# Turning the order of the maxima units and spreading V's products over the period, in a fused attention and mixture-of-experts kernel

## What is computed

```python
q = _apply_rope(q, cos, sin); k = _apply_rope(k, cos, sin)
scores = jnp.einsum('bhsd,bhtd->bhst', q, k) / scale
scores = jnp.where(causal, scores, -inf)
attn = softmax(scores)
out = jnp.einsum('bhst,bhtd->bhsd', attn, v)
```

## Time and profile before

| | |
|---|---|
| median of 3 runs | 180.74 us (180.57 to 181.24) |
| profiled execution, its own time | 180.87 us |
| its span in the trace | 179.1 us |
| busy in the span | PE 95%, VectorE 77%, ACT 75%, POOL 52% |
| granted TensorE clock | 1.00 in every slice |
| attention periods 1 to 6 | 34.67 to 83.47 us |

### The profile page before, as it was taken

How to read it: one execution, slowest core, us unless ns; L and a number is a source line. 1 busy time by engine, 2 the same in 40 slices (tenths; PEclk the granted TensorE clock), 3 DMA queues, 4 the chain that set the end, 5 groups by cost and what they waited for, 6 DMA issues and landing times.

```text
span 179.1 us, 3277 instructions
## 1 busy us (share of the span) xinstructions
PE 169.9 (95%) x944; PEld 117.8 (66%) x944; DVE 138.5 (77%) x444; ACT 134.6 (75%) x224; POOL 93.2 (52%) x117
## 2 busy tenths in 40 slices
PE   6999999899999999988999999987999999999992
PEld 2766675565666666654648777855777877788881
DVE  5598989889898989981586998898699748657561
ACT  3559267687777888889735696944979999999970
POOL 5507187985453969597541632004569941777000
PEclk9999999999999999999999999999999999999999
DMA  5924673677686657521120899970680000001001
GB/s 126 310 48 100 180 197 88 213 264 267 173 239 202 186 183 187 151 88 43 59 55 9 214 322 354 344 216 9 170 297 3 0 4 0 0 2 59 0 4 59
DMA packets 15349, 24.28 MB, mean 136 GB/s; under 512 B 2844, under 2 KB 4828, under 8 KB 15308
## 3 DMA queue, kind: packets, MB, share of 16 engines
q1 hardware_dynamic: 14532, 23.29, 42.9%
q10 hardware_dynamic: 800, 0.79, 1.6%
HBM read 18.71 MB, written 5.27 MB: 134 GB/s over the span
## 4 chain that ended last, share of the span: by engine, by line
PE 77%; DVE 10%; ACT 5%; POOL 3%; issue 3%; DVEq 0%; POOLq 0%
PE psum L1544 12%; PE psum L1545 11%; PE psum L1546 11%; PE psum L1411 10%; PE psum L1471 8%; PE psum L1447 7%; PE psum L1290 4%; PE psum L1356 2%; PE psum L1342 2%; ACT t_probs L1109 2%; DVE psum L776 2%; PE psum L1406 1%; PE psum L1451 1%; DVE t_raw L928 1%; PE psum L1300 1%
## 5 line engine op out<-in xcount | busy, mean ns | idle before, releaser
L776 DVE CUSTOM_DVE_ANT_0 psum<-psum,t_causal 128x128 f32<-128x128 f32 (+3 forms) x128 | 58.5, 524 | 5.7 <-PE psum L1411 3.0
L1109 ACT ACTIVATE t_probs<-psum 128x1024 f32<-128x1024 f32 (+2 forms) x48 | 40.9, 884 | 8.2 <-PE psum L1447 5.2
L1411 PE MATMUL psum<-t_stacked,t_q_pad 96*128 96x256 f32 (+2 forms) x104 | 33.3, 391 | 0.5 <-DMA t_q_pad<-scratch 0.2
L1411 PEld LDWEIGHTS psum<-t_stacked,t_q_pad 96*128 96x128 f32 x104 | 18.4, 189 | 12.4 <-DVE t_row_max L776 10.1
L948 DVE SCALAR_TENSOR_TENSOR t_q_pad<-psum,t_zw_all,t_q_pad 128x512 fp32r<-128x512 f32 x24 | 17.8, 748 | 9.9 <-ACT t_q_pad L1157 9.9
L676 POOL TENSOR_SCALAR_AFFINE_SELECT t_probs<-t_probs 128x512 f32<-128x512 f32 x32 | 20.4, 649 | 9.0 <-ACT t_probs L1109 9.0
L1143 ACT ACTIVATE psum<-psum 128x512 f32<-128x512 f32 x40 | 23.5, 587 | 0.4 <-DVE t_q_pad L951 0.2
L707 POOL TENSOR_TENSOR t_q_pad<-t_raw,t_q_pad 128x512 fp32r<-128x512 f32 x8 | 10.3, 1294 | 21.6 <-ACT t_q_pad L1159 21.6
L1471 PE MATMUL psum<-t_probs,t_v_all 128*32 128x512 f32 (+3 forms) x256 | 20.6, 439 | 0.0
L776 DVE DVE_READ_ACCUMULATOR2_ANT t_row_max<- 128x1 f32 x128 | 18.0, 140 | 0.0
L1157 ACT ACTIVATE t_q_pad<-psum,t_zw_all 128x512 fp32r<-128x512 f32 x24 | 16.6, 691 | 0.9 <-PE psum L1546 0.2
(11 more groups left out here) (233 smaller groups left out, 372.0 us busy)
## 6 DMA issues: line engine op xcount, KB each, us to landing
t_stacked<-scratch SPq DMA_DIRECT2D x16, 256.0 KB, 5.8
t_probs<-in_L_ffn_Wa SPq DMA_DIRECT2D x2, 1024.0 KB, 12.4
scratch<-t_o_sb SPq DMA_DIRECT2D x7, 256.0 KB, 2.0
t_raw<-in_experts SPq DMA_DIRECT2D x7, 256.0 KB, 3.1
t_stacked<-scratch SPq DMA_DIRECT2D x9, 192.0 KB, 3.4
t_q_pad<-scratch SPq DMA_DIRECT2D x28, 48.0 KB
scratch<-t_dn_hi SPq DMA_DIRECT2D x2, 512.0 KB, 3.3
t_q_two<-scratch SPq DMA_DIRECT2D x5, 192.0 KB, 2.5
```

The costliest lines, as they stand in the source:

```text
L776: last = V.tensor_tensor_reduce(scores, scores, causal[:, S - width:S], 1.0, 3 * BIG, ALU.add, ALU.max, row_max[s][:, qb, j:j + 1])
L1109: A.activation(o, scores, ACT.Exp, scale=float(1.0 / np.sqrt(np.float32(HD)))).then_inc(exp_done, 1)
L1411: last = T.matmul(bank[:, o:o + width], q_pad[s][0:TOP, j, qb * P:(qb + 1) * P], stacked[0:TOP, n, 0:width], start=True, stop=True)
```

## The change

1. Groups 3 to 7 take their maxima units in a turned order: F F F, H H, T, D, T T T, F. Group 2 keeps its order.
2. `LEAD` is 6 instead of 7.
3. In the PE loop the score units 3 and 4 stand between other slices, and `weigh_v(n, 0)` moves from before slice 7 to behind slice 9. The last period is written out for itself, with its old order.
4. In periods 1 to 6 POOL places the maxima ahead of its wait for exponential 3.
5. POOL's list of period 0 is turned: the last queries come ahead of `turn(1)`, whose two products are split over two places; `turned(1)` goes behind the masks of the last pair.
6. One low part of batch 1 (`take_late_low(0)`) goes to VectorE, behind maxima unit (2, 3); the other stays on POOL, after the last queries of group 1.
7. ACT's `split_high` of a period's first chunk moves ahead of `copy_pv`.

```diff
-MX_UNITS = [SPREAD_UNITS if n < 2 else PAIRED_UNITS for n in range(GROUPS)]
+TURNED_UNITS = FOUR[0:3] + HEAD_PAIRS + THREE[0:1] + DIAGONAL + THREE[1:4] + FOUR[3:4]
+MX_UNITS = [SPREAD_UNITS if n < 2 else PAIRED_UNITS if n == 2 else TURNED_UNITS for n in range(GROUPS)]
...
-LEAD, FIRST = 7, 4
+LEAD, FIRST = 6, 4
...
+LATE_LOW = (2, 3)
...
-                    sp.wait_ge(mx_full, units_to(n - 1) if n < 4 else units_to(n - 1) - 1)
+                    sp.wait_ge(mx_full, units_to(n - 1) - (n == 4))
...
+                    if c == 1 and 1 <= n < GROUPS - 1:
+                        place_max(n + 1)
                     pool.wait_ge(exp_done, STU * n + 2 * c + 2)
-                    if c == 1 and n + 1 < GROUPS:
+                    if c == 1 and n == 0:
                         place_max(n + 1)
...
+                    if n == 0 and c == 0:
+                        spread_last_queries(0)
+                        turn(1, 0)
+                    if n == 0 and c == 1:
+                        turn(1, 1)
+                    if n == 0 and c == 2:
+                        turned(1)
                     if c == 2 and n + 1 < GROUPS:
                         spread_last_queries(n + 1)
...
+                    if n == 0 and c == 2:
+                        pool.wait_ge(lo_ready, 5)
+                        take_late_low(1)
...
+            def take_late_low(i):
+
+                dve.wait_ge(hi_ready, 4 + i + 1)
+                dve.wait_ge(rep_ready, 2 * BY_PE + 2)
+                for written in spilled:
+                    dve.wait_ge(written, 16 * SPILLS)
+                V.tensor_tensor(qk_lo[:, i, :], roped[:, i, :], f32_of(qk_hi[:, i, :]),
                                 ALU.subtract).then_inc(lo_ready, 1)
...
+                if (n, u) == LATE_LOW:
+                    take_late_low(0)
...
+                if (n, 0) in SPLITS:
+                    split_high(SPLITS[n, 0])
                 if 0 < n < GROUPS - 1:
                     copy_pv(n - 1)
                 exp(n, 2)
                 if n == 0:
                     copy_v(1)
-                if (n, 0) in SPLITS:
-                    split_high(SPLITS[n, 0])
...
                 maximum(3)
                 scores_for_exp(n, 2)
-                scores_for_exp(n, 3)
                 maximum(4)
                 maximum(5)
+                scores_for_exp(n, 3)
                 maximum(6)
                 scores_for_exp(n, 4)
-                weigh_v(n, 0, 0, S)
                 maximum(7)
                 lay_max_under_q(n + 1)
                 maximum(8)
                 scores_for_exp(n, 5)
                 maximum(9)
+                weigh_v(n, 0, 0, S)
                 maximum(10)
```

More of the change, by code:

```diff
@@ L36 @@
 SPREAD_UNITS = [[(j, qb, i * 2 * P) for i, qb in enumerate(blocks)] for blocks in ((0, 1), (2,), (3,)) for j in range(HG)]
-PAIRED_UNITS = [[(2 * h2 + i, 1, i * 2 * P) for i in range(2)] for h2 in range(2)]
-PAIRED_UNITS += [[(j, qb, 0)] for qb in (2, 3) for j in range(HG)] + [[(j, 0, j * P) for j in range(HG)]]
-MX_UNITS = [SPREAD_UNITS if n < 2 else PAIRED_UNITS for n in range(GROUPS)]
+HEAD_PAIRS = [[(2 * h2 + i, 1, i * 2 * P) for i in range(2)] for h2 in range(2)]
+THREE, FOUR = [[[(j, qb, 0)] for j in range(HG)] for qb in (2, 3)]
+DIAGONAL = [[(j, 0, j * P) for j in range(HG)]]
+PAIRED_UNITS = HEAD_PAIRS + THREE + FOUR + DIAGONAL
+TURNED_UNITS = FOUR[0:3] + HEAD_PAIRS + THREE[0:1] + DIAGONAL + THREE[1:4] + FOUR[3:4]
+MX_UNITS = [SPREAD_UNITS if n < 2 else PAIRED_UNITS if n == 2 else TURNED_UNITS for n in range(GROUPS)]
 MX_LIST = [(n, u) for n in range(GROUPS) for u in range(len(MX_UNITS[n]))]
@@ L623, in split_low, with turn @@
                                 ALU.subtract).then_inc(w_lo, 1)
-            def turn(i):
+            def turn(i, t):
                 pool.wait_ge(pj_copied, i + 1)
@@ L629, in turn @@
                     pool.wait_ge(m_ready, 1)
[L630 to L633, removed]
+                o = (rope_c[i], rope_s[i])[t]
+                G.tensor_tensor(o.rearrange("p (h c) -> p h c", h=2),
+                                unrot[:, 2 * i + t, :].rearrange("p (h c) -> p h c", h=2),
+                                turns[:, :, t, :], ALU.mult).then_inc(rope_ready, 1)
+            def take_late_low(i):
+                pool.wait_ge(hi_ready, 4 + i + 1)
+                pool.wait_ge(rep_ready, 2 * BY_PE + 2)
+                for written in spilled:
+                    pool.wait_ge(written, 16 * SPILLS)
+                G.tensor_tensor(qk_lo[:, i, :], roped[:, i, :], f32_of(qk_hi[:, i, :]),
+                                ALU.subtract).then_inc(lo_ready, 1)
             def turned(i):
@@ L664, in spread_last_queries @@
                                 ALU.mult).then_inc(q_last_ready, 1)
-            turn(0)
+            turn(0, 0)
+            turn(0, 1)
             turned(0)
@@ L1631, in zone_spread @@
                 T.matmul(sum_bank(b)[:, 80:80 + TOPZ], ones_row[:], zw[:, b, :], start=True, stop=True).then_inc(z_bc, 1)
-            for n in range(GROUPS):
+            for n in range(GROUPS - 1):
                 def maximum(i):
@@ L1650, in _ @@
                 scores_for_exp(n, 2)
[L1651 to L1653 removed]
                 maximum(4)
                 maximum(5)
+                scores_for_exp(n, 3)
                 maximum(6)
                 scores_for_exp(n, 4)
[L1658 to L1660 removed]
                 maximum(7)
[L1662 to L1663 removed]
+                lay_max_under_q(n + 1)
                 maximum(8)
@@ L1666, in _ @@
                 maximum(9)
+                weigh_v(n, 0, 0, S)
                 maximum(10)
+            last = GROUPS - 1
+            scores_for_exp(last, 0)
+            scores_for_exp(last, 1)
+            weigh_v(last - 1, 1, P, S)
+            weigh_v(last - 1, 2, 2 * P, S)
+            weigh_v(last - 1, 3, 3 * P, S)
+            scores_for_exp(last, 2)
+            project_out(0)
+            scores_for_exp(last, 3)
+            scores_for_exp(last, 4)
+            route_experts(0)
+            weigh_v(last, 0, 0, S)
+            scores_for_exp(last, 5)
             up(0)
```

## The result

| | before | after |
|---|---|---|
| median of 20 runs each | 180.75 us (180.20 to 181.72) | 180.32 us (178.72 to 182.61) |
| ratio | | 0.9939, interval 0.992 to 0.9959 |
| profiled execution, its own time | 180.87 us | 179.45 us |
| its span | 179.1 us | 177.6 us |

The change makes the kernel faster by 0.6%, 1.1 us by the ratio. That is less than half of the 2.4 us forecast, and the median lies just above the range.

The account below looks back on a forecast made before the run. The order bounds it: TensorE (7.74 us) and VectorE (7.16) stall each other to 8.23 a period. Gains of 0.75 + 4 x 0.32 + 0.4 make 2.4 us, giving 178.3 us; its own range 177.7 to 178.9, overall 177.2 to 180.3.

Parts of the forecast that it names:

- Periods 2 to 6 and the end: From slice 9's H at 40.6 to the end: periods of 7.9, group 7's scores at 81.0 against 83.47, 2.4 us gained.
- 0.35 us late in ACT's queue: Period 6: last expert chunk's load lands late for ACT, delaying the copy, exponentials 2 to 4 and the maxima copy.
- I pass the 2.4 us on whole: Tail after group 7's scores: every step hangs on their start, so the whole 2.4 us gain reaches the end.
- Period 1: From group 1's scores at 34.0 to group 2's at 42.1 to 42.2, VectorE-fed; 0.75 us gained against 42.91.
- comes at 40.6: Period 1: TensorE reaches slice 9's H at 40.6, with everything behind the V block fed by VectorE.
- Taken at full size it puts POOL's chain 0.5 us back: POOL's masks slowed by VectorE's subtraction: 0.5 us of room left at q_pad(4) instead of 1.0, total time unchanged.
- Steady periods: Periods 2 to 5: TensorE's 7.73 us plus 0.18 exposure at the laying gives 7.9, 0.32 less than 8.23.
- 0.1 before TensorE wants its slot: Steady period on ACT: exponential 2 ends at 6.2, so ACT is close but behind and adds no wait.
- Period 6: Only F is left of the maxima; the chunk's wait delays ACT, and the period contributes 0.4 us of the gain.
- (a): Rival: the laying is not exposed, the period is TensorE's 7.73, 0.9 us more is won: 177.4 us; chance 17%.
- (b): Rival: late transfers, q_pad(4), q_pad(7) and the expert chunk, eat the gain: 180.2 us; chance, wholly or partly, 18%.
- (c): Rival: slower by POOL, whose placing behind low split and mask holds TensorE's laying; 182.3 us with periods of 8.9; chance 10%.

Follow-up runs that it names:

- experiment 4: Changed kernel with ACT's copy of V's sums (`copy_pv`) behind exponential 2 instead of ahead of it: 181.39 us, ratio 1.0025 to the kernel before.
- 8: Changed kernel with groups 3 to 7 back in the old order of maxima units: 182.64 us, ratio 1.0094 to the kernel before.
- experiment 9: Changed kernel with V's first part back ahead of slice 7 in every period: 183.11 us, ratio 1.0108 to the kernel before.
- experiment 2: Changed kernel with VectorE's low part cut to one column of 512, the rest not computed: 180.02 us, ratio 0.9933 to the kernel before.
- experiment 1: The changed kernel once more, nothing altered, beside the kernel before: 180.54 us, ratio 0.996.
- experiment 3: Changed kernel with POOL's placing of the maxima back behind its wait for exponential 3: 182.03 us, ratio 1.0064 to the kernel before.
- 6: Changed kernel with V's first part ahead of the laying in period 6, last expert chunk left late: 180.61 us, ratio 0.9972 to the kernel before.
- 5: Changed kernel with the last expert chunk loaded in SP's pass 3, with chunks 4 and 5: 179.9 us, ratio 0.9945 to the kernel before.
- experiment 7: Changed kernel with the last chunk in SP's pass 3 and V's first part ahead of period 6's laying: 180.62 us, ratio 0.9982 to the kernel before.
- 10: Changed kernel with the last expert chunk issued in SP's pass 4 ahead of the inverse's store: 179.1 us, ratio 0.9899 to the kernel before.
- experiment 11: As 10, with VectorE's inverse product behind unit 8 of group 7 instead of the last unit: 179.49 us, ratio 0.9938 to the kernel before.
- experiment 12: As 10, with VectorE's low part behind maxima unit (2, 1) instead of (2, 3): 179.99 us, ratio 0.9947 to the kernel before.

## Why the prediction was wrong, and where it was right

The forecast was 178.3 us, the median is 180.32. Half of the 2.0 us shows in the profiled execution (179.45 against 178.45), the other half is scatter that the kernel before does not have. So two things failed, of about one size.

**The step that failed behind the scatter** is in "Periods 2 to 6 and the end": the chunk "lands at 76.8, while ACT now wants it at 76.3: 0.35 us late in ACT's queue", and with it "I pass the 2.4 us on whole". The lateness was seen and its sign was right, but it was priced from one landing time, the 3.1 us of the trace before (and 76.8 less 76.3 is 0.5, not 0.35). With the chunk in its late place the load landed 2.7 us from its issue in the profile after, 3.0 in that of experiment 4, 3.4 in 8, 4.6 in 9, 5.0 and 5.05 in 2 and 1, and 5.4 in 3 and 6. With 2.7 ACT waits 0.53 us, which cost nothing, since the path through VectorE and the placing is as long; with 5.0 and more it waits up to 1.85, and period 6 grows by 0.87 in experiment 1. Before the change ACT took this chunk at 80.45; issued at 74.95 it would have been there at 80.35 even with 5.4 us, so every landing was hidden. The change took that cover away. Behind a late landing there is a dearer thing: TensorE stands still for about 1.5 us, and in some executions its clock then falls to 0.50 for some 3 us, which costs about 1 us more. The clusters lie at 179.4, 180.8 and about 182 us.

How far this is shown: the wait and its price stand in the traces. The fallen clock went with the chunk moved: it is in 7 of the 32 runs of the change (the result's and experiment 1's) and in 6 of the 37 of the four experiments that keep the late chunk and the new places (2, 3, 4, 6), but in none of 52 with the chunk moved (5, 7, 10 to 12). But on the chips of experiments 5 to 12 only 2 of 21 runs with the late chunk have it, so part of this may be the chip. That TensorE's standstill brings the fall on is what its place in the traces says; no run forces it. In the profile of experiment 3 it came behind standstills of 0.85 and 0.54 us in the same place, and in that of experiment 9 in period 1, behind two stalls of 0.3 us and far from the chunk.

In the medians the chunk's share is less sure. Against the kernel before they gain 0.43 and 0.33 us with the late chunk (the result and experiment 1), and 0.87, 1.89, 1.50 and 1.00 with the chunk moved (5, 10, 11, 12), but experiments 6 and 7, on one chip, gain 0.16 with the late chunk and 0.15 with the moved one. Runs over 180.5 us at full clock are 9 of the change's 25, and still 12 of the 52 with the chunk moved, six of them in experiment 7 and four in 11. So the chunk is not the whole scatter, and the rest stays open. Waits for q_pad (below) and for VectorE's low part (1.18 us in the profiles of experiments 1 and 3, 0.69 in the profile after) also come and go between executions. A wait in the tail for `t_stacked` from DRAM (4.79 us from issue in the profile of experiment 7) is a candidate; it was not tried.

**The terms of the sum that were mis-sized**, from the profiled execution, 0.97 us at group 7's scores (81.97 against 81.0):

- *Period 1*, +0.50. Forecast from 34.0 to about 42.15, measured 33.97 to 42.62. I had it fed by VectorE alone, by which slice 9's H "comes at 40.6" (measured 40.96, and 41.04 in experiment 2, where VectorE does feed it). The start of that path was right ("Its F behind the V block arrives at 37.6": 37.65 measured), but the sentence has no term for what stands behind VectorE's last reduction: in experiment 2 that ends at 39.50, and placing and laying take until 40.52. Nor did I add anything for POOL and ACT; in the chain of the profile after they are `turned` 1.26, high part 0.62, exponential 0.92, copy 0.47, exponential 0.72, unit 4. "Taken at full size it puts POOL's chain 0.5 us back [...]; the sum is unchanged" was right about POOL's size (1.75 against 1.22 us for two masks) and, by experiment 2, nearly right about the sum for POOL's part, but only because a second path is as long; that VectorE pays instead in some executions (1.18 instead of 0.69 us in experiment 1, 0.3 us in period 1) was not thought of.
- *Steady periods*, 8.0 instead of 7.9: +0.39 in four. The laying's exposure was 0.08, and the H behind it took 0.05 more, together less than the 0.18 taken. Not counted was unit 4's wait for exponential 2 (0.13), which the text had as a tie ("0.1 before TensorE wants its slot").
- *Period 6*, +0.11 (7.36). The forecast took the chunk's wait for what sets it. The chain goes through F's reduction, the slowed placing (0.55 instead of 0.20) and the laying; with the chunk early it is as long (experiments 5 and 10), and with the placing short it is 7.19 (experiment 11).

**Right:** group 1's scores at 33.97 (34.0) and the wait for `spread_last_queries` gone; the period bounded by TensorE's own sum; VectorE's longest idle, 0.5 us, ahead of a 384-column reduction behind the long V block; POOL's placing waits for VectorE (1.04 us), no longer for ACT; the tail is 95.63 us. The turned units, V's place and the early placing are each needed: without one of them the kernel is 0.6 to 1.1% slower than before (experiments 3, 8, 9).

**Rivals.** (a) did not come: the exposures are 0.26. (b) was right in kind, and I gave it 18%: 180.2 from late transfers is close to the median. Its q_pad part is absent from the profile after, but not from the changed kernel's kin: TensorE waits for q_pad(7) in the profiles of experiments 4, 5 and 7, about 0.4 us or more on period 5 each, the first with the chunk not moved, and weight loads wait for a q_pad in those of 1 (0.15 us) and 11 (0.32, on q_pad(4)). Its weight was too low because I asked of each transfer how long it takes, not how much that varies. (c) did not come: POOL idles 1 us a period before the placing.

## What to carry to other kernels

When a change makes a stage shorter, list the loads that end in it by how much room each still has, and price them by the slowest landing of such a transfer, not by the one that the profile happened to catch. Ask also whether the wait ends on the longest path: here 0.53 us of it cost nothing, 1.42 us cost 0.87. A load with nothing to wait for is best moved ahead at once, to a place in the queue where it delays nothing. Look at the spread of the runs as well as the median: clusters that the kernel before does not have mean a wait that is there only in some executions, and a second profile may find it. Where two paths of equal length end a stage, undo one alone before believing that its cost counts.

## What was unexpected of the hardware

- **A 256 KB load landed 2.7 or 5.05 us after its issue in two executions of one kernel**, and the one issued earlier (73.76 against 74.81) landed later. In the late case it stood 0.6 us behind a store of the same size instead of 1.9, and the data moved mostly by 77 us (131 GB/s in the slice from 76, 25 and 8 in the next two), with a few packets trickling to 78.8. What holds these back was not tried.
- **TensorE's granted clock fell to 0.50 (1.2 GHz) inside a kernel that is otherwise at 1.00**, behind standstills of 1.56 and 1.90 us, once behind 0.85 and 0.54 and once behind two of 0.3, but not behind one of 1.46 (experiment 1) or 0.57 (after). The Trainium skill (TensorE: Matmul & The Clock Gate, Part 1) says that the clock hangs on how busy TensorE has been and names these two levels; the windows of experiment 2 agree.
- **Two engines slow each other, and in these traces the one that started later pays**: a POOL mask beside a VectorE operation with two SBUF inputs takes 1.14 or 1.09 instead of 0.63 us, and POOL's 16-column copy 0.55 instead of 0.20, each begun 0.04 to 0.4 us behind VectorE's. In experiment 12 POOL's product of two tiles began 0.18 us ahead of VectorE's subtraction: POOL keeps its 1.28 us, and VectorE takes 1.65 instead of 0.69. In experiment 9 the subtraction began 0.75 us behind the first of two masks and took 1.01; the masks kept their 1.22. Where subtraction and masks began within 0.03 us of each other, VectorE kept its 0.69 and the masks took 1.75 in eight profiles, but in those of experiments 1 and 3 both were long (1.18, and 1.67 or 1.68). No run changed the order of starts alone. The Trainium skill (GPSIMD Engine Reference, Specifications) names the contention and gives no size there.
